# Self-attention and a circular channel filter: the sum of both channel tiles in place of x's first tile, and separate logarithms and shifts for each half of the positions

## The chip, the cores and the metric

The kernel runs on one core of one Trainium2 chip. The metric is device microseconds of one execution; the shown time is the median of three runs.

## What is computed

x has 16 images of 256 channels and 32 x 32 positions. Each image goes through a self-attention and then through a filter across channels:

```
theta = theta_w x            (32 x 1024)      phi = pool2(phi_w x)   (32 x 256)
g     = pool2(g_w x)         (128 x 256)      beta = softmax(theta^T phi)
z     = gamma * (o_w (g beta^T)) + x
out   = z + T z              T: 256 x 256, circular, 26 taps, 13 to either side
```

pool2 is the maximum over 2 x 2 positions. T plus the identity is called the band below. Because the band is circular and the channels form two tiles of 128, it has only two different blocks: the diagonal block D, the same for both tiles, and the corner block E (13 channels reach over each border), the same in both directions. So out0 = D x0 + E x1 and out1 = D x1 + E x0, with the attention part added to each.

## The kernel before

Nothing is computed in less than float32 accuracy: every operand is split into a high part (float32r, rounded) and a low part (the rest), and a product is three matmuls, high by high, high by low and low by high (`three`). Positions go in two halves h of 512 columns, channels in two tiles t (as input) or f (as output).

`over_images` runs a function `image(i, par)` on each engine, with i the pair and par the image in it. In each call PE finishes the attention of image n = (i, par) and makes the projections and scores of image n+1 (`following`). The order on each engine is written out by hand, with semaphore waits between engines:

- PE: `g_transposed` of image n (two small transposes, at the end of the call before), `scores_transposed(h)` (the probabilities' exponents, transposed, with the softmax shift as additional rows), `g_projection(n+1, h)` of 6 matmuls, `theta_phi(n+1, h)` of 4, `filter_x(h, f)` of 4 (three for the diagonal block, one for the corner: 78 stacked rows `x_edge` of the other tile), `attention_input_high/low` (4 and 2), `scores(n+1, h)`, and for each h, f `add_high_attention` (2) and `add_low_attention` (1). A turn has 64 matmuls of 512 columns, 8 of 256 and the two transposes.
- ACT: evacuations and roundings, exponentials of the scores for the sums (`exp_sums`), one logarithm of all 8 sums (`ln_sums`), `probabilities`, and `x_high`, the rounding of the image after next. It copies the results (h, f) = (1, 1) and (1, 0) out of PSUM.
- DVE: sums, pools, low parts, the maxima, the copies of (0, 1) and (0, 0) out of PSUM, and the shifts: `shifts` makes neg_max minus logarithm and its two parts (128 x 8), `turn_shifts` turns them by four 32 x 32 transposes, and `spread_shifts` writes them into rows of `theta_aug`, masked by `own_tile`, once for each half.
- POOL: `x_low` (2 a turn) and `prob_low` (2 a turn).
- SP: loads two images ahead, stores, and copies of the edge rows (`x_edges`, 6 DMAs an image).

`scores_transposed(h)` waits for the rows of `spread_shifts`; `g_transposed` waits for the evacuation of result (1, 1) of the image before, `g_projection(h=0)` for (1, 0); `theta_phi(h=1)` waits for `sum_thetaphi(h=0)`. The first two images have another order, written out separately.

Of the kernel before, what the change touches and what calls it, by code (L numbers as in the profile page):

```python
# [11 lines left out]
P = 128  # L34


def attention_then_channel_filter(nc, x, proj_wT, o_w, gamma, ring, out):
# [12 lines left out]
    K_AUG = R_SHIFT + SHIFT_ROWS  # L50
    SQUARE = 32
# [9 lines left out]
    with ExitStack() as ctx:  # L61
# [9 lines left out]
        g_raw = proj_raw[:, :, 2 * K:2 * K + CG]  # L71
        tp_w = sb("tp_w", [P, CT, 4, K], F32R)
        g_hi_w = sb("g_hi_w", [P, CT, CG], F32R)
# [8 lines left out]
        edge_w = sb("edge_w", [K_EDGE, CT * P], F32R)  # L82
        w2_hi = sb("w2_hi", [P, C], F32R)
# [40 lines left out]
        shift_turned_ps = psZ[:, 1, 4 * NT:4 * NT + P]  # L124
# [3 lines left out]
        first_ln_sum_ps = [ps[:, 1, 0:NT] for ps in scores_ps]  # L128
        first_shift_sum_ps = [ps[:, 1, NT:2 * NT] for ps in scores_ps]
# [20 lines left out]
        w2_hi_ready = sem("w2_hi_ready")  # L150
        w2_ready = sem("w2_ready")
# [51 lines left out]
        shift_turned = sem("shift_turned")  # L203
# [27 lines left out]

        def following(i, par):
            return (i, 1) if par == 0 else (i + 1, 0)
# [4 lines left out]
        def over_images(engine, image):  # L238

            image(0, 0)  # L240
            image(0, 1)
            with engine.Fori(1, PAIRS - 1) as i:
                image(i, 0)
                image(i, 1)
            image(PAIRS - 1, 0)
            image(PAIRS - 1, 1)
# [7 lines left out]
        def has_next_but_one(i, par):  # L254
            return not (is_number(i) and i == PAIRS - 1)

# [46 lines left out]
        def _(sp):  # L303
# [30 lines left out]
            def x_edges(i, par):  # L334
                for h in range(2):
                    sp.wait_ge(x_lo_ready[h], from_second(1, i, par, 1))
                stack_edges(x_edge[:, par], x_edge_loaded[par], (x_hi[:, par], x_hi[:, par], x_lo[:, par]))
# [26 lines left out]
            def image(i, par):  # L364
# [10 lines left out]
                else:  # L375
                    for h, f in ((0, 0), (0, 1), (1, 0)):
# [10 lines left out]
        def _(pool):  # L387
# [64 lines left out]

            def prob_low(i, par, h):
# [6 lines left out]
            own_tiles()  # L460
            x0_low(1, 1)
            phi0_copy(0)
            pool.wait_ge(phi0_lo_ready, 2)
# [8 lines left out]
            edge_weights()  # L472
            prob_low(0, 0, 0)
            prob_low(0, 0, 1)
            x_low(1, 0, 0)
            x_low(1, 0, 1)

            def image(i, par):
# [14 lines left out]
        def _(act):  # L493
# [5 lines left out]
            def x_high(i, par, h):  # L499
                cols = slice(h * HALF, (h + 1) * HALF)  # L500
                act.wait_ge(x_loaded[h][par], 16 * (i + par))
                if not is_second(i, par):
# [18 lines left out]
            def exp_sums(i, par, h):  # L521
                act.wait_ge(neg_max_ready, from_second(2, i, par, h + 1))
                tiles = scores_ps[h][:, :, :].rearrange("p a (b m) -> p (a b) m", m=M)
                for t in range(NT):
# [3 lines left out]
                last.then_inc(exp_sum_ready, 1)  # L528
# [72 lines left out]
            def ln_sums0(h):  # L601
                act.wait_ge(exp_sum_ready, h + 1)
                nc.scalar.activation(first_ln_sum_ps[h], exp_sum[:, h * NT:(h + 1) * NT], ACT.Ln).then_inc(ln_sum0_ready, 1)
# [40 lines left out]
            def image(i, par):  # L644
# [41 lines left out]
        def _(dve):  # L686
# [41 lines left out]
            def split_phi(i, par):  # L728
# [4 lines left out]
                else:  # L733
                    for rows in (slice(0, K), slice(2 * K, 3 * K)):
                        nc.vector.tensor_copy(phi_aug[rows, par, :], phi_pool[:]).then_inc(phi_hi_ready, 1)
# [596 lines left out]
```

## Time and profile before

| | us |
|---|---|
| median of three runs (272.91 to 273.39) | 273.18 |
| span of the profiled execution, first to last instruction | 271.3 |
| PE busy | 265.4 (98%) |
| DVE busy | 245.9 (91%) |
| ACT busy | 243.2 (90%) |
| POOL busy | 149.6 (55%) |

Busy times count an instruction from its start to its end, and neighbouring instructions of one engine overlap a little. So the work of an engine is better read from the distance between starts. About 1.9 us of the time lie outside the span.

### The profile page before, as it was taken

The numbers are of one execution on the slowest core, as the hardware profiler recorded it, in microseconds if no ns is written. First come the engines' busy times: TensorE is split into PE (matmuls) and PEld (weight loads), VectorE is DVE, ScalarE is ACT, GpSimd is POOL, SyncE is SP. The second block draws the span as 40 slices with busy tenths as digits, with TensorE's granted clock in tenths as the row PEclk, the third lists the DMA queues.
The fourth block names the chain that finished last, engine by engine and source line by source line (L and its number), as shares of the span: only waits on it lengthen the run. The fifth ranks groups of instructions, "written<-read, shape, count | busy, mean of one in ns | idle before, by whom it ended". The sixth has DMA issues, their size and how long they took to land.

```text
span 271.3 us, 4464 instructions
## 1 busy us (share of the span) xinstructions
PE 265.4 (98%) x1196; PEld 211.8 (78%) x1196; DVE 245.9 (91%) x456; ACT 243.2 (90%) x533; POOL 149.6 (55%) x79
## 2 busy tenths in 40 slices
PE   7999999999999999999999999999999999999994
PEld 3576778888888888888888888888887888888873
DVE  4998999999999999999999999999999999999953
ACT  4999999999999999998999999999999989998772
POOL 1585747574565747546673764667466475745100
PEclk9999999999999999999999999999999999999999
DMA  7978085582847657284673828467283855317044
GB/s 198 270 208 212 23 234 169 175 223 81 193 142 225 180 170 182 88 218 149 203 201 144 180 79 246 157 197 206 98 182 124 234 169 172 77 71 178 1 157 155
DMA packets 17380, 44.57 MB, mean 164 GB/s; under 512 B 2654, under 2 KB 3578, under 8 KB 16122
## 3 DMA queue, kind: packets, MB, share of 16 engines
q1 hardware_dynamic: 16682, 44.00, 56.4%
q10 hardware_dynamic: 688, 0.46, 0.5%
q8 instruction: 4, 0.07, 0.1%
q14 instruction: 6, 0.05, 0.1%
HBM read 17.45 MB, written 16.78 MB: 126 GB/s over the span
## 4 chain that ended last, share of the span: by engine, by line
PE 94%; DVE 2%; DMA 2%; ACT 0%; issue 0%; SPq 0%
PE psY L1009 10%; PE psY L988 8%; PE psY L990 7%; PE psY L989 7%; PE psV L1128 6%; PE psY L1112 6%; PE psY L1128 5%; PE psV L1112 5%; PE psV L988 3%; PE psV L990 3%; PE psV L989 3%; PE psX L1066 3%; PE psV L1096 3%; PE psV L1133 3%; PE psZ L1066 3%; PE psY L1118 3%
## 5 line engine op out<-in xcount | busy, mean ns | idle before, releaser
L457 POOL TENSOR_TENSOR prob_lo<-prob,prob_hi 128x1024 fp32r<-128x1024 f32 x30 | 72.1, 2404 | 59.7 <-ACT prob L537 32.5
L450 POOL TENSOR_TENSOR x_lo<-x_raw,x_hi 128x1024 fp32r<-128x1024 f32 x30 | 72.0, 2399 | 35.5 <-ACT x_hi L504 34.0
L504 ACT CAST x_hi<-x_raw 128x1024 fp32r<-128x1024 f32 x30 | 31.5, 1052 | 6.8 <-PE psY L1096 5.2
L526 ACT ACTIVATE psX<-psX,neg_max 128x256 f32<-128x256 f32 x60 | 26.7, 445 | 3.0 <-DVE neg_max L777 3.0
L526 ACT ACTIVATE psZ<-psZ,neg_max 128x256 f32<-128x256 f32 x60 | 27.4, 468 | 0.0
L709 DVE TENSOR_TENSOR thetaphi<-psY,thetaphi_rest 64x512 f32<-64x512 f32 x30 | 20.5, 682 | 3.8 <-ACT thetaphi_rest L508 3.1
L988 PE MATMUL psY<-x_hi,g_hi_w 128*128 128x512 f32 x56 | 22.2, 396 | 0.0
L990 PE MATMUL psY<-x_hi,g_lo_w 128*128 128x512 f32 x56 | 22.0, 393 | 0.0
L989 PE MATMUL psY<-x_lo,g_hi_w 128*128 128x512 f32 x56 | 22.0, 392 | 0.0
L715 DVE TENSOR_TENSOR theta_aug<-thetaphi,theta_aug 32x512 fp32r<-32x512 f32 x30 | 20.5, 683 | 0.9
L702 DVE TENSOR_REDUCE phi_pool<-thetaphi 32x128 f32<-32x512 f32 x30 | 20.2, 674 | 1.0
L702 DVE TENSOR_REDUCE g_pool<-psY 128x128 f32<-128x512 f32 x28 | 19.4, 692 | 0.9
L508 ACT COPY thetaphi_rest<-psY 64x512 f32<-64x512 f32 x30 | 17.5, 583 | 1.7 <-PE psY L1009 0.5
L1009 PE MATMUL psY<-x_hi,tp_w 128*128 128x512 f32 x60 | 18.9, 396 | 0.0
L777 DVE TENSOR_REDUCE neg_max<-psX 128x4 f32<-128x1024 f32 x15 | 18.3, 1217 | 0.6 <-PE psX L1050 0.6
L1009 PE MATMUL psY<-x_lo,tp_w 128*128 128x512 f32 x60 | 18.8, 394 | 0.0
L817 DVE TENSOR_TENSOR theta_aug<-psZ,own_tile 16x512 fp32r<-16x512 f32 x28 | 17.9, 678 | 0.5
L777 DVE TENSOR_REDUCE neg_max<-psZ 128x4 f32<-128x1024 f32 x15 | 18.2, 1213 | 0.0
L513 ACT CAST theta_aug<-thetaphi 32x512 fp32r<-32x512 f32 x30 | 18.1, 602 | 0.0
L519 ACT CAST theta_aug<-thetaphi 32x512 fp32r<-32x512 f32 x30 | 17.2, 617 | 0.4
L542 ACT ACTIVATE prob_hi<-psZ 128x1024 fp32r<-128x1024 f32 x16 | 16.4, 1027 | 0.4
L542 ACT ACTIVATE prob_hi<-psX 128x1024 fp32r<-128x1024 f32 x16 | 16.5, 1032 | 0.1
(189 smaller groups left out, 766.1 us busy)
## 6 DMA issues: line engine op xcount, KB each, us to landing
x_raw<-x SPq DMA_DIRECT2D x30, 512.0 KB, 5.1
out<-y SPq DMA_DIRECT2D x15, 1024.0 KB, 4.0
x_edge<-x_hi SPq DMA_DIRECT2D x64, 104.0 KB
x_edge<-x_lo SPq DMA_DIRECT2D x32, 104.0 KB
x_raw<-x SPq DMA_DIRECT2D x4, 256.0 KB, 4.5
out<-y SPq DMA_DIRECT2D x3, 256.0 KB, 2.1
band_rev<-ring SPq DMA_DIRECT2D x2, 128.0 KB, 6.9
out<-y ACTq DMA_DIRECT2D x1, 256.0 KB, 2.6
```

What stands on the lines that cost most here:

```text
L450: nc.gpsimd.tensor_tensor(x_lo[:, par, :, cols], x_raw[:, par, :, cols], x_hi[:, par, :, cols].bitcast(F32), ALU.subtract).then_inc(x_lo_r ...
L457: nc.gpsimd.tensor_tensor(prob_lo[:, h], prob[:, h], prob_hi[:, h].bitcast(F32), ALU.subtract).then_inc(prob_lo_ready, 1)
L504: nc.scalar.copy(x_hi[:, par, :, cols], x_raw[:, par, :, cols]).then_inc(x_hi_ready[h], 1)
L526: last = nc.scalar.activation(tiles[:, t, :], tiles[:, t, :], ACT.Exp, bias=neg_max[:, col:col + 1], accum_out=exp_sum[:, col:col + 1])
L542: nc.scalar.activation(prob_hi[:, h], scores_ps[h][:, :, :], ACT.Exp).then_inc(prob_hi_ready, 1)
L702: return nc.vector.tensor_reduce(dst.rearrange("p (r c) -> p r c", c=SIDE // 2), src.rearrange("p (r a c b) -> p r c a b", a=2, b=2, c=SID ...
L777: nc.vector.tensor_reduce(neg_max[:, h * NT:(h + 1) * NT], tiles, AXIS.X, ALU.max, negate=True).then_inc(neg_max_ready, 1)
L988: nc.tensor.matmul(dst, wh, vh, start=first, stop=False)
L989: nc.tensor.matmul(dst, wh, vl, start=False, stop=False)
L990: return nc.tensor.matmul(dst, wl, vh, start=False, stop=last)
L1009: last = nc.tensor.matmul(thetaphi_bank(i, par, h), tp_w[:, t].rearrange("p a k -> p (a k)"), part[:, par, t, cols], start=part is x_hi an ...
L1112: nc.tensor.matmul(o_in_bank(i, par, h), g_part[:, t, :], prob_hi[:, h, t, :], start=t == 0 and g_part is gT_hi, stop=False)
```

## The change

For all images but the first two, x0 is replaced in place by u = x0 + x1 (`add_tiles`, on POOL, once per half). With u, the sum of both outputs is S = out0 + out1 = (D + E) u, which needs no corner, and out1 = (D - E) x1 + E u. PE makes S in the bank of f = 0 and out1 in that of f = 1, and DVE writes out0 = S - out1 (`rest_of_sum`). The weights follow: for tile 1 of the projections the difference of the two tiles' weights, for S the sum of both tiles' attention weights, and the sum and difference of D and E. They are made once, by POOL, in the first 50 us. The edge rows are needed for one tile alone, so each of the 6 DMAs is half as large.

The second part: the logarithm, the shift and its parts are made for each half (`ln_half`, `half_shifts`), and a matmul by the identity (`half_shifts_to_rows`) turns each half's 8 rows, in place of the four transposes. Around this the order on ACT, DVE and PE is rewritten. One copy out of PSUM changes places: ACT takes (0, 1) in place of (1, 0), and `rest_of_sum` for h = 1 is DVE's.

```diff
+            def add_tiles(i, par, h):
+                cols = slice(h * HALF, (h + 1) * HALF)
+                pool.wait_ge(x_loaded[h][par], 16 * (i + par))
+                nc.gpsimd.tensor_tensor(x_raw[:, par, 0, cols], x_raw[:, par, 0, cols], x_raw[:, par, 1, cols], ALU.add).then_inc(u_ready[h], 1)
...
@@ POOL, image @@
-                    for h in range(2):
-                        pool.wait_ge(theta_lo_ready, upto(2, *following(i, par), h + 1))
-                        prob_low(i, par, h)
-                if has_next_but_one(i, par):
-                    for h in range(2):
+                    pool.wait_ge(theta_lo_ready, upto(2, *following(i, par), 1))
+                    prob_low(i, par, 0)
+                    pool.wait_ge(theta_lo_ready, upto(2, *following(i, par), 2))
+                    pool.wait_ge(phi_ready, from_second(1, *following(i, par), 1))
+                    prob_low(i, par, 1)
+                for h in range(2):
+                    if has_next_but_one(i, par):
                         x_low(i + 1, par, h)
+                    if has_next_but_two(i, par):
+                        ni, npar = following(i, par)
+                        add_tiles(ni + 1, npar, h)
...
@@ ACT, image @@
                     theta_high(ni, npar, 1)
+                    theta_copy(ni, npar, 0)
                 probabilities(i, par, 1)
...
-                for h in range(2):
-                    theta_copy(ni, npar, h)
+                o_in_high(i, par, 0)
+                theta_copy(ni, npar, 1)
                     x_high(i + 1, par, 0)
-                o_in_high(i, par, 0)
-                for h in range(2):
-                    exp_sums(ni, npar, h)
-                ln_sums(ni, npar)
+                out_of_psum(i, par, 0, 1)
+                exp_sums(ni, npar, 0)
+                exp_sums(ni, npar, 1, 0, 1)
+                ln_half(ni, npar, 0)
+                exp_sums(ni, npar, 1, 1, NT)
                     x_high(i + 1, par, 1)
-                for f in (1, 0):
-                    out_of_psum(i, par, 1, f)
+                ln_half(ni, npar, 1)
+                out_of_psum(i, par, 1, 1)
...
@@ DVE @@
+            def rest_of_sum(i, par, h):
+                cols = slice(h * HALF, (h + 1) * HALF)
+                dve.wait_ge(out_evacuated[h][1], upto(1, i, par, 1))
+                dve.wait_ge(out_done[h][0], upto(1, i, par, 1))
+                dve.wait_ge(y_stored[par], 16 * i)
+                nc.vector.tensor_tensor(y[:, par, 0, cols], out_bank(i, par, h, 0), y[:, par, 1, cols],
+                                        ALU.subtract).then_inc(out_evacuated[h][0], 1)
...
                 sum_thetaphi(ni, npar, 0)
+                gT_low(i, par)
                 pool_phi(ni, npar, 0)
-                gT_low(i, par)
...
-                split_phi(ni, npar)
+                round_phi(ni, npar)
                 theta_low(ni, npar, 1)
+                low_phi(ni, npar)
                 pool_g(ni, npar, 1)
+                o_in_low(i, par, 0)
                 maxima(ni, npar, 0)
-                o_in_low(i, par, 0)
                 maxima(ni, npar, 1)
-                out_of_psum(i, par, 0, 1)
                 o_in_high(i, par, 1)
-                out_of_psum(i, par, 0, 0)
+                half_shifts(ni, npar, 0)
                 o_in_low(i, par, 1)
-                shifts(ni, npar)
-                turn_shifts(ni, npar)
-                for h in range(2):
-                    spread_shifts(ni, npar, h)
+                rest_of_sum(i, par, 0)
+                half_shift_rows(ni, npar, 0)
+                half_shifts(ni, npar, 1)
+                rest_of_sum(i, par, 1)
+                half_shift_rows(ni, npar, 1)
...
@@ PE @@
+            def half_shifts_to_rows(i, par, h):
+                pe.wait_ge(half_shift_parts_ready, from_third(2, i, par, h + 1))
+                nc.tensor.matmul(half_shift_ps[h], shift_parts[:, h * NT:(h + 1) * NT, :].rearrange("p t s -> p (t s)"), ident_r[:],
+                                 start=True, stop=True).then_inc(half_shift_rows_done, 1)
...
+                last = three(out_bank(i, par, h, f), diagonal_parts, x_parts(par, f, h), True, False)
+                if f == 0 and not is_raw(i):
+                    last.then_inc(x_used[h], 1)
+                    return
...
                 g_projection(ni, npar, 1)
+                attention_input_low(i, par, 0)
                 filter_x(i, par, 0, 1)
                 scores(ni, npar, 0)
-                attention_input_low(i, par, 0)
+                add_high_attention(i, par, 0, 1)
+                add_low_attention(i, par, 0, 1)
                 scores(ni, npar, 1)
+                add_high_attention(i, par, 0, 0)
                 attention_input_high(i, par, 1)
-                for f in (1, 0):
-                    add_high_attention(i, par, 0, f)
-                add_low_attention(i, par, 0, 1)
                 attention_input_low(i, par, 1)
                 add_low_attention(i, par, 0, 0)
+                filter_x(i, par, 1, 0)
                 filter_x(i, par, 1, 1)
-                filter_x(i, par, 1, 0)
-                for f in (1, 0):
-                    add_high_attention(i, par, 1, f)
-                for f in (1, 0):
-                    add_low_attention(i, par, 1, f)
+                add_high_attention(i, par, 1, 0)
+                half_shifts_to_rows(ni, npar, 0)
+                add_high_attention(i, par, 1, 1)
+                add_low_attention(i, par, 1, 1)
+                add_low_attention(i, par, 1, 0)
...
                 g_transposed(ni, npar)
+                half_shifts_to_rows(ni, npar, 1)
```

## Rows read from the trace of the kernel before

**Rows 1.** The page: span, busy time of each engine, and PE's granted clock.
```profile
span 271.3 us, 4464 instructions
...
PE 265.4 (98%) x1196; PEld 211.8 (78%) x1196; DVE 245.9 (91%) x456; ACT 243.2 (90%) x533; POOL 149.6 (55%) x79
...
PEclk9999999999999999999999999999999999999999
```

**Rows 2.** Timeline of PE: start, duration, engine, line, operation, tiles, count.
```profile
33.04 0.38 PE L1035 MATMUL psV<-ident,g_pool 128*128 128x128 f32 x2
...
141.28 0.39 PE L988 MATMUL psV<-x_hi,band_hi 128*128 128x512 f32 x1
...
144.53 0.63 PE L1009 MATMUL psY<-x_hi,tp_w 128*128 128x512 f32 x2
...
257.83 0.38 PE L1035 MATMUL psV<-ident,g_pool 128*128 128x128 f32 x2
```

**Rows 3.** Timeline of PE at the first image's shift product.
```profile
18.88 0.22 PE L1186 MATMUL psZ<-ident_r,shift_parts 128*16 128x128 f32 x1
18.94 0.44 PE L988 MATMUL psV<-x_hi,g_hi_w 128*128 128x512 f32 x1
```

**Rows 4.** Timeline of DVE over one turn; brackets show idle time before and its releaser.
```profile
142.59 0.68 DVE L757 TENSOR_TENSOR o_in_lo<-psY,o_in_hi 128x512 fp32r<-128x512 f32 x1
...
143.78 0.90 DVE L809 STREAM_TRANSPOSE psZ<-shift_parts 32x32 f32<-32x32 f32 x4
144.72 1.28 DVE L817 TENSOR_TENSOR theta_aug<-psZ,own_tile 16x512 fp32r<-16x512 f32 x2
146.28 0.68 DVE L709 TENSOR_TENSOR thetaphi<-psY,thetaphi_rest 64x512 f32<-64x512 f32 x1 [0.28 <-ACT thetaphi_rest L508]
147.00 0.68 DVE L702 TENSOR_REDUCE phi_pool<-thetaphi 32x128 f32<-32x512 f32 x1
147.70 0.42 DVE L748 TENSOR_TENSOR gT_lo<-psV,gT_hi 128x256 fp32r<-128x256 f32 x1
148.16 0.68 DVE L715 TENSOR_TENSOR theta_aug<-thetaphi,theta_aug 32x512 fp32r<-32x512 f32 x1
148.87 0.69 DVE L702 TENSOR_REDUCE g_pool<-psY 128x128 f32<-128x512 f32 x1
...
151.04 0.94 DVE L735 CAST phi_aug<-phi_pool 32x256 fp32r<-32x256 f32 x2
152.01 0.41 DVE L737 TENSOR_TENSOR phi_aug<-phi_pool,phi_aug 32x256 fp32r<-32x256 f32 x1
152.46 0.68 DVE L715 TENSOR_TENSOR theta_aug<-thetaphi,theta_aug 32x512 fp32r<-32x512 f32 x1
```

**Rows 5.** Timeline of DVE in the first images.
```profile
21.05 0.67 DVE L709 TENSOR_TENSOR thetaphi<-psY,thetaphi_rest 64x512 f32<-64x512 f32 x1
21.65 0.67 DVE L702 TENSOR_REDUCE g_pool<-psV 128x128 f32<-128x512 f32 x1
22.36 0.68 DVE L702 TENSOR_REDUCE phi_pool<-thetaphi 32x128 f32<-32x512 f32 x1
```

**Rows 6.** Timeline of ACT at the end of the same turn.
```profile
143.40 1.05 ACT L504 CAST x_hi<-x_raw 128x1024 fp32r<-128x1024 f32 x1 [0.37 <-PE psY L1096]
```

**Rows 7.** POOL: timeline of one turn.
```profile
144.53 2.40 POOL L450 TENSOR_TENSOR x_lo<-x_raw,x_hi 128x1024 fp32r<-128x1024 f32 x1 [2.51 <-ACT x_hi L504]
149.12 2.40 POOL L457 TENSOR_TENSOR prob_lo<-prob,prob_hi 128x1024 fp32r<-128x1024 f32 x1 [2.19 <-ACT prob L537]
```

**Rows 8.** POOL: the only half-size subtraction, from the groups by line (busy, mean ns).
```profile
L407 POOL TENSOR_TENSOR x_lo<-x_raw,x_hi 128x512 fp32r<-128x512 f32 x1 | 1.3, 1263 | 5.9 <-ACT x_hi L563 5.9
```

**Rows 9.** Durations of DVE's rounding of phi: min/median/max ns.
```profile
L735 DVE CAST phi_aug<-phi_pool x28: 284/430/658, 39.0 to 248.1; 32x256 fp32r<-32x256 f32 x28
```

**Rows 10.** Timeline of the end: the last evacuation and its store.
```profile
267.57 0.58 ACT L557 COPY y<-psV 128x512 f32<-128x512 f32 x1 [0.82 <-PE psV L1133]
268.19 0.37 ACTq L665 DMA_DIRECT2D out<-y  x1
```

More of the change, by code:

```diff
@@ L241, in over_images @@
             image(0, 1)
-            with engine.Fori(1, PAIRS - 1) as i:
+            with engine.Fori(1, PAIRS - 2) as i:
                 image(i, 0)
                 image(i, 1)
-            image(PAIRS - 1, 0)
-            image(PAIRS - 1, 1)
+            for i in (PAIRS - 2, PAIRS - 1):
+                image(i, 0)
+                image(i, 1)
         def is_number(i):
@@ L255, in has_next_but_one, with has_next_but_two, is_raw @@
             return not (is_number(i) and i == PAIRS - 1)
+        def has_next_but_two(i, par):
+            return not is_number(i) or 2 * i + par + 3 < B
+        def is_raw(i):
+            return is_number(i) and i == 0
         def is_last(i, par):
@@ L519, in theta_copy, with exp_sums @@
                 nc.scalar.copy(theta_aug[K:2 * K, par, h * HALF:(h + 1) * HALF], thetaphi[0:K, h, :]).then_inc(theta_copied, 1)
-            def exp_sums(i, par, h):
+            def exp_sums(i, par, h, first=0, end=NT):
                 act.wait_ge(neg_max_ready, from_second(2, i, par, h + 1))
                 tiles = scores_ps[h][:, :, :].rearrange("p a (b m) -> p (a b) m", m=M)
-                for t in range(NT):
+                for t in range(first, end):
                     col = h * NT + t
@@ L527, in exp_sums, with ln_half @@
                                                 bias=neg_max[:, col:col + 1], accum_out=exp_sum[:, col:col + 1])
-                last.then_inc(exp_sum_ready, 1)
+                if end == NT:
+                    last.then_inc(exp_sum_ready, 1)
+            def ln_half(i, par, h):
+                act.wait_ge(exp_sum_ready, upto(2, i, par, h + 1))
+                nc.scalar.activation(half_ln_sum_ps[h], exp_sum[:, h * NT:(h + 1) * NT], ACT.Ln).then_inc(half_ln_sum_ready, 1)
             def ln_sums(i, par):
@@ L735, in split_phi, with low_phi @@
                         nc.vector.tensor_copy(phi_aug[rows, par, :], phi_pool[:]).then_inc(phi_hi_ready, 1)
+            def low_phi(i, par):
+                if not is_second(i, par):
                     dve.wait_ge(phi_hi_ready, from_second(2, i, par, 1))
@@ new lines, in half_shift_rows @@
+            def half_shift_rows(i, par, h):
+                dve.wait_ge(half_shift_rows_done, from_third(2, i, par, h + 1))
+                row = half_shift_ps[h].rearrange("r (o n) -> r o n", o=1).broadcast_to([2 * NT, NT, P])
+                own = own_tile[0:2 * NT, 0:NT].rearrange("r (t o) -> r t o", o=1).broadcast_to([2 * NT, NT, P])
+                rows = theta_aug[R_SHIFT:K_HALF, par, h * HALF:(h + 1) * HALF].rearrange("r (t n) -> r t n", n=P)
+                nc.vector.tensor_tensor(rows, row, own, ALU.mult).then_inc(shift_rows_ready, 1)
@@ L1003, in theta_phi @@
                     pe.wait_ge(thetaphi_summed, from_second(2, i, par, 1))
+                if is_number(i) and (i, par, h) == (1, 0, 0):
+                    pe.wait_ge(proj_dw_ready, 2)
+                weights = [tp_w[:, 0], tp_w[:, 1] if is_raw(i) else tp_dw[:]]
                 cols = slice(h * HALF, (h + 1) * HALF)
@@ L1022, in g_projection @@
                 for t in range(CT):
-                    last = three(g_bank(i, par, h), (g_hi_w[:, t, :], g_lo_w[:, t, :]), x_parts(par, t, h), t == 0, t == CT - 1)
+                    weights = (g_hi_w[:, t, :], g_lo_w[:, t, :]) if t == 0 or is_raw(i) else (g_hi_dw[:], g_lo_dw[:])
+                    last = three(g_bank(i, par, h), weights, x_parts(par, t, h), t == 0, t == CT - 1)
                 last.then_inc(g_done, 1)
```

173 lines of the change are left out of this document (130 added, 43 removed).

## The prediction

> **What bounds the kernel now.** I read the page first. PE is busy 98% of the span at full clock, with DVE at 91%, ACT at 90% and POOL at 55% [rows 1]: PE comes first, but two engines follow closely. The timeline of PE then gives the turn of one image. From the transposes of the second image (33.04) to those of the last (257.83) are 224.79 us and 14 turns, 16.06 each [rows 2]. Inside, 14 products of 512 columns start between 141.28 and 144.53, one each 0.232 us [rows 2]. A turn of 64 such products, 8 half-wide ones (as 4) and the transposes is 15.8 and a remainder of 0.3: PE hardly waits anywhere. So only what leaves PE's list can save time, as long as DVE and ACT keep up. The timeline of DVE shows how near DVE is: over a whole turn one marked wait of 0.28, in front of the sum at 146.28 [rows 4]. ACT shows one of 0.37, in front of the rounding of x [rows 6]. The question is thus not what PE saves, but who sets the turn afterwards.
>
> **PE alone.** The corner of f = 0 goes in 14 images and both halves: 28 products by 0.232 = 6.5 us. 28 shift products come. In the first image one of them starts at 18.88 and the next product at 18.94, which is then 0.05 longer than the usual 0.39 [rows 3]: 0.11 each, 3.1 us. Were PE all, a turn would be 16.06 - 0.46 + 0.22 = 15.82 and the kernel 3.4 us faster. The bounds of a shift product are 0.06 and 0.22, its duration [rows 3]; this moves the sum by 1.4 us down and 3.1 up.
>
> **DVE's work.** Removed are four transposes, 0.94 from start to start [rows 4]. Three small shift instructions of some 0.2 each become six, +0.6. The two copies out of PSUM become two subtractions with one operand in PSUM; the nearest row is o_in_low, 0.68 long [rows 4], which is what a copy of that size takes (0.58 on ACT [rows 10]). So DVE has 0.3 less work, a turn of some 15.4 without waits. That fits under 15.82. But DVE's new list now waits on three others within a turn: on PE for the turned rows, on ACT for each logarithm and for the evacuation of f = 1 that each subtraction reads.
>
> What a step costs on DVE I take from starts, and the rows show two kinds. Where an instruction starts on the same partitions as those before it, it begins 0.08 before the end of its forerunner: the sum at 21.05 is 0.67 long and the pool follows after 0.60 [rows 5]. Where the partitions change, or the instruction needs its forerunner's result, it begins 0.03 to 0.04 after the end: pool after 0.71 [rows 5], theta_low (0.68) followed after 0.71, gT_low (0.42) after 0.46 [rows 4]. The new order turns two of the slow steps into fast ones: gT_low stands directly behind the sum (0.60 in place of 0.72), and theta_low(1) behind the rounding of phi, whose last output starts on the same partitions (0.87 in place of 0.97 for the pair [rows 4]). No row shows the second one; its bounds are these two, and I take 0.87. The Trainium skill, VectorE: DVE Perf Modes, section "Two Vector instructions with no wait between them", has this as a rule of quadrants of 32 partitions: an instruction that starts in another quadrant than the last reads and write is held until all earlier ones have finished. Rows 4 and 5 agree with it; without the fast step the ring below would be 0.1 longer.
>
> **The ring that sets the new turn.** The new order makes a closed chain through DVE and PE. It begins with half_shift_rows(1), which needs PE's shift product of half 1, placed behind the transposes. On DVE follow, by starts: half_shift_rows 0.72 (the pair at 144.72 is 1.28 long, so one is 0.68 and a change of partitions 0.04), sum 0.60, gT_low 0.46, pool_phi 0.71, theta_low 0.71, pool_g 0.61, sum 0.72, pool_phi 0.71, rounding pair 0.87, theta_low 0.71, low_phi 0.45 (152.01 to 152.46), pool_g 0.61, and o_in_low(0) with its whole 0.68 [rows 4, 5]. That is 8.56. Then PE's add_low_attention(0, 1), which the new order has early, can go: I take 0.16, the gap of 0.04 of a dependent step and half a product for the weight load (bounds 0.04 and 0.23). From there to the transposes PE has 27 products and the scores of half 1 (as 2): 29 by 0.232 = 6.73. One shift product, 0.11, and 0.4 for the transposes and the end of the next shift product make it 7.2, and 0.04 leads back to DVE. The sum is 8.56 + 0.16 + 7.2 + 0.04 = 15.96. I add 0.04 for one of the short waits on ACT that the list has (such as the 0.28 at 146.28 [rows 4]), which makes 16.0. So not PE's 15.82, but the ring's 16.0 would be the turn: 0.06 less than now. Over the 13 turns from the third image on, -0.8 us. The other ring, from the maxima of half 0 over ACT's exponentials, x_high(1) and the second logarithm back to half_shifts(1), comes out a little shorter, by 0.1 or so.
>
> **POOL.** add_tiles is 28 additions of 1.26 each [rows 8]. With 4 instructions of 2.40 a turn [rows 7] POOL has 12.1 of 16: it fits, and the load two images ahead is there in time. Hidden, as long as add_tiles(1) is over when DVE wants to go on (see the rivals). The difference weights are made in POOL's idle time at the start: 0, at most 0.6 (half an add_tiles that ACT's x_high must wait for in the second image). I take 0, since DVE is the later one there. The halved edge copies are hidden before and after: 0.
>
> **The end.** The last image has both scores_transposed directly behind each other. The second now needs half_shift_rows(1), which starts only after the transposes and the shift product: 0.4, then 0.04 + 0.68, then 0.16, is 1.3 us after the transposes' start, and with the ring's delay up to 1.5, where PE would be ready at 0.8. +0.6. The last image's two corners are saved, -0.46. The last store was issued at 268.19, behind ACT's copy that started at 267.57 [rows 10]. Now ACT's copy is first (0.23 earlier, as PE finishes f = 1 first), and DVE's subtraction follows it: 267.34 + 0.58 + 0.04 + 0.68 = 268.64, and the issue 268.7. +0.5.
>
> **The sum.** -0.8 + 0.6 - 0.46 + 0.5 = -0.16. On the profiled execution (271.3 and 1.9 outside, 273.2) this is 273.0, and the median of the runs, 273.18, is the same time: I forecast 273.0.
>
> **Rivals.** (A) The ring is shorter than I sum it, and PE stays the bound. Its length is thirteen steps of 0.5 to 0.9 with an error of a few hundredths each; 0.15 less would do. For it: PE's list loses 0.24 and DVE's 0.3. Against it: PE is dependent on o_in_low(0) six products earlier than now. Then 13 turns by 0.24 = -3.1, -0.46 and +0.5 as above, +0.4 at the last scores: -2.7, 270.5. Halfway, 271.8.
>
> (B) Slower: add_tiles(1) holds DVE. Now x_low(1) runs from 144.53 to 146.93, and theta_low(0), with both operands in SBUF, starts at 148.16 [rows 4, 7]: 1.23 between them, where add_tiles(1) of 1.26 comes. That such overlaps cost is in the rows: the two roundings of phi that start while prob_low runs (149.12 to 151.52) take 0.94, and one alone at best 0.284; the longest took 0.658 [rows 4, 7, 9]. In the new order theta_low(0) is some 0.25 later against the transposes, so by my timeline add_tiles(1) ends 0.2 before it. If ACT's x_high(1) is later than now by more than that, theta_low(0), which stands on the ring, is held by the excess. At 0.15 a turn the 13 turns cost 2.0: 275.0. It decides from 2.9 us after the transposes' start on, as the end of add_tiles(1). The Trainium skill, SBUF — State Buffer, section "Who interferes with whom", speaks for this rival: a DVE instruction with two SBUF inputs and a GpSimd instruction that reads SBUF exclude each other, and the second one blocks fully; rows 9 agree. By it the hold would be up to the whole 1.26.
>
> (C) The ring is longer by 0.1 (theta_low(1) not early, or PE's start after a wait 0.23): 16.1, a turn as now. Then the end's +0.64 remains: 273.9.
>
> **Chances.** My forecast, with the ring between 15.96 and 16.05, 272.4 to 273.6: 0.40, a fifth of it under 272.6. (A), with what lies between: 0.33. (B) and (C) together: 0.27, nearly all over 273.7. A measurement of this kernel can tell 0.2%, 0.55 us, from no change. Faster 0.41, same 0.33, slower 0.26. The range takes in (A) whole and (B) at 0.15: 270.3 to 275.3.
>
> **What the profile would show.** PE has 28 corner products fewer and some marked waits on DVE o_in_lo in front of add_low_attention(0, 1), none now; the distance of the transposes is 16.0 (15.8 in A, over 16.1 in B). DVE waits in front of o_in_high(1) and half_shifts. half_shift_rows(1) starts 0.4 to 0.5 after the transposes. In (B) theta_low is longer than 0.68 on the mean, or idle before it. At the end the last DVE instruction is a subtraction behind ACT's copy. I am wrong if the turn is under 15.9 or over 16.1.

## The result and the profile after

The changed kernel takes 277.80 us (median of 4 runs, 277.70 to 277.85) beside 273.28 for the kernel before on the same chip: a ratio of 1.0148, 95% interval 1.0113 to 1.0183 (the two medians alone give 1.0165, inside it). The forecast was 273.0 with a range up to 275.3; the time lies above it. The page of the changed kernel, answering to [rows 1]:

```profile
span 276.1 us, 4480 instructions
...
PE 266.0 (96%) x1196; PEld 205.7 (74%) x1196; DVE 244.3 (88%) x442; ACT 245.6 (89%) x547; POOL 191.3 (69%) x120
...
PEclk9999999999999999999999999999999999999999
...
L515 POOL TENSOR_TENSOR x_raw<-x_raw 128x512 f32<-128x512 f32 x28 | 36.6, 1308 | 0.0
```

The granted clock is full and PE's busy time hardly moved, yet its share fell from 98% to 96%: PE now waits somewhere. POOL is the engine with much more work, 41.7 us, 36.6 of it the 28 additions of the tiles (1308 ns each on the mean, where the estimate was 1.26 us). The first thing to find is where in the span the 4.8 us are. The transposes of g stand once in each turn, so their starts on PE's timeline cut the span into pieces, as in [rows 2]:

```profile
35.08 0.44 PE L1150 MATMUL psV<-ident,g_pool 128*128 128x128 f32 x2
...
53.05 0.38 PE L1150 MATMUL psV<-ident,g_pool 128*128 128x128 f32 x2
...
69.22 0.38 PE L1150 MATMUL psV<-ident,g_pool 128*128 128x128 f32 x2
...
261.60 0.38 PE L1150 MATMUL psV<-ident,g_pool 128*128 128x128 f32 x2
```

| | before | after | difference |
|---|---|---|---|
| first image's transposes | 16.24 | 16.67 | +0.43 |
| from there to the second image's | 16.80 | 18.41 | +1.61 |
| first turn, to the third image's | 16.19 | 17.97 | +1.78 |
| the 13 turns from there | 208.60 | 208.55 | -0.05 |
| last transposes to the end | 13.47 | 14.50 | +1.03 |
| span | 271.3 | 276.1 | +4.8 |

So 3.82 of 4.8 us are lost before the third image's transposes, 1.03 at the end, and nothing on balance in the thirteen turns that the prediction spent most of its words on.

**The start.** PE's marked waits from 20 us to the third image's transposes, in the changed kernel:

```profile
23.40 0.50 PE L1099 MATMUL psV<-x_hi,band_hi 128*128 128x512 f32 x1 [0.91 <-DVE w_lo L998]
...
27.08 0.71 PE L1165 MATMUL psX<-phi_aug,theta_aug 96*128 96x256 f32 x4 [0.53 <-DVE phi_aug L830]
...
44.72 0.72 PE L1165 MATMUL psX<-phi_aug,theta_aug 96*128 96x256 f32 x4 [1.04 <-DVE phi_aug L830]
```

They name DVE, and DVE is not idle there: single instructions of it are far too long (w_lo in the rows is what `w2_low` writes). DVE's timeline of the changed kernel at the first and third of these places:

```profile
21.09 2.25 DVE L998 TENSOR_TENSOR w_lo<-w_raw,w_hi 128x256 fp32r<-128x256 f32 x1
...
40.91 2.51 DVE L825 CAST phi_aug<-phi_pool 32x256 fp32r<-32x256 f32 x2
```

The same two places in the kernel before:

```profile
20.66 0.47 DVE L894 SCALAR_TENSOR_TENSOR w_lo<-psV,gamma_sb,w_hi 128x256 fp32r<-128x256 f32 x1
...
39.03 0.89 DVE L735 CAST phi_aug<-phi_pool 32x256 fp32r<-32x256 f32 x2
```

And POOL's timeline of the changed kernel says what ran meanwhile:

```profile
20.67 2.38 POOL L521 TENSOR_TENSOR prob_lo<-prob,prob_hi 128x1024 fp32r<-128x1024 f32 x1 [0.34 <-ACT prob L625]
...
36.98 1.31 POOL L515 TENSOR_TENSOR x_raw<-x_raw 128x512 f32<-128x512 f32 x1
38.24 0.94 POOL L502 TENSOR_TENSOR band_c<-band 128x128 f32<-128x128 f32 x1
39.14 0.46 POOL L503 TENSOR_TENSOR band_c<-band 128x128 f32<-128x128 f32 x1
39.56 2.40 POOL L521 TENSOR_TENSOR prob_lo<-prob,prob_hi 128x1024 fp32r<-128x1024 f32 x1
41.93 1.34 POOL L515 TENSOR_TENSOR x_raw<-x_raw 128x512 f32<-128x512 f32 x1
```

w2_low used to read its product from PSUM and took 0.47 us. In the changed kernel both its inputs lie in SBUF; it starts 0.42 after prob_low(0, 0, 0), and ends at 23.34, 0.29 after prob_low does (23.05). The two roundings of phi start at 40.91 inside prob_low(0, 1, 0), which comes late because three additions stand ahead of it, and end only after the addition that follows it on POOL has run as well. This is rival (B)'s mechanism, at places where the prediction did not look.

The 0.43 that are already there at the first image's transposes come from one more such place, at 6 us. The first two rows are DVE's and POOL's in the changed kernel, the last is DVE's in the kernel before:

```profile
6.08 1.12 DVE L931 TENSOR_TENSOR x_lo<-x_raw,x_hi 128x512 fp32r<-128x512 f32 x1 [0.41 <-ACT x_hi L651]
```

```profile
6.07 0.59 POOL L477 TENSOR_TENSOR proj_d<-proj_raw 128x192 f32<-128x192 f32 x1 [3.98 <-DMA proj_raw<-proj_wT]
```

```profile
6.13 0.69 DVE L827 TENSOR_TENSOR x_lo<-x_raw,x_hi 128x512 fp32r<-128x512 f32 x1 [0.43 <-ACT x_hi L563]
```

The POOL instruction is the difference of the projections' weights, which the prediction put at 0. In every changed kernel below it runs beside this low part of x, which then takes 0.87 to 1.12; in the two kernels without it, 0.69. No experiment moved it. So the 3.82 read as 0.43 here, 1.61 mainly at w2_low (1.78 too long), and 1.78 in the first turn (the roundings are 1.62 too long).

**The turn.** DVE's timeline of one changed turn, from half_shift_rows(1) to o_in_low(0), and PE's product that waits for it; it answers to [rows 4]:

```profile
150.04 0.68 DVE L921 TENSOR_TENSOR theta_aug<-psZ,own_tile 8x512 fp32r<-8x512 f32 x1
150.76 0.68 DVE L799 TENSOR_TENSOR thetaphi<-psY,thetaphi_rest 64x512 f32<-64x512 f32 x1
151.37 0.41 DVE L841 TENSOR_TENSOR gT_lo<-psV,gT_hi 128x256 fp32r<-128x256 f32 x1
...
152.51 0.68 DVE L805 TENSOR_TENSOR theta_aug<-thetaphi,theta_aug 32x512 fp32r<-32x512 f32 x1
...
155.25 1.03 DVE L825 CAST phi_aug<-phi_pool 32x256 fp32r<-32x256 f32 x2
156.20 0.68 DVE L805 TENSOR_TENSOR theta_aug<-thetaphi,theta_aug 32x512 fp32r<-32x512 f32 x1
...
157.97 0.68 DVE L850 TENSOR_TENSOR o_in_lo<-psV,o_in_hi 128x512 fp32r<-128x512 f32 x1
```

```profile
158.70 0.50 PE L1264 MATMUL psY<-o_in_lo,w_hi 128*128 128x512 f32 x1
```

From 150.04 to the end of o_in_low(0), 158.65, are 8.61; the prediction had 8.56. PE follows 0.05 later. theta_low(0) is 0.68, not held. This is a turn of 16.15; in every other one the first rounding is 0.14 shorter and the same stretch is 8.46 long. The waits of the changed kernel, in total, times and longest:

```profile
PEld psY L1264 <- DVE o_in_lo L850: 5.1, 14, 0.4
```

PE waits 0.36 in each turn at the forecast place.

**The end.** PE's second scores of the last image, first in the kernel before, then in the changed one, and then the last evacuations of the changed one:

```profile
258.51 0.65 PE L1066 MATMUL psZ<-theta_aug,phi_aug 112*128 112x512 f32 x2
```

```profile
262.94 0.73 PE L1188 MATMUL psZ<-theta_aug,phi_aug 104*128 104x512 f32 x2 [0.39 <-DVE theta_aug L921]
...
271.63 0.59 ACT L645 COPY y<-psV 128x512 f32<-128x512 f32 x1 [0.81 <-PE psV L1264]
272.25 0.69 DVE L866 TENSOR_TENSOR y<-psY,y 128x512 f32<-128x512 f32 x1 [0.71 <-ACT y L645]
```

The second scores start 1.34 after the transposes (0.68 before), +0.66. The last evacuation is the subtraction behind ACT's copy, as forecast.

### The profile page after: what moved, and what is told of

The parts are those of the page before. It is cut to its first block, busy times and chain, and to the rows that moved or that the text cites. A ratio compares the mean times of both kernels' runs of the same rounds, so it can differ in the third digit from the quotient of the medians.

```text
span 276.1 us, 4480 instructions
## 1 busy us (share of the span) xinstructions
PE 266.0 (96%) x1196; PEld 205.7 (74%) x1196; DVE 244.3 (88%) x442; ACT 245.6 (89%) x547; POOL 191.3 (69%) x120
## 4 chain that ended last, share of the span: by engine, by line
PE 84%; DVE 11%; DMA 2%; issue 1%; ACT 1%; SPq 0%; DVEq 0%
PE psY L1123 9%; PE psY L1099 7%; PE psY L1100 7%; PE psY L1101 7%; PE psV L1258 6%; PE psY L1258 5%; PE psY L1241 5%; PE psV L1241 4%; PE psY L1264 3%; PE psX L1165 3%; PE psV L1264 3%; PE psZ L1165 3%; PE psY L1247 3%; PE psV L1101 3%; PE psV L1099 3%; PE psV L1100 3%
## 5 line engine op out<-in xcount | busy, mean ns | idle before, releaser
L515 POOL TENSOR_TENSOR x_raw<-x_raw 128x512 f32<-128x512 f32 x28 | 36.6, 1308 | 0.0
L602 ACT CAST theta_aug<-thetaphi 32x512 fp32r<-32x512 f32 x30 | 18.6, 620 | 0.7
L596 ACT CAST theta_aug<-thetaphi 32x512 fp32r<-32x512 f32 x30 | 18.1, 602 | 0.5 <-DVE thetaphi L799 0.5
L846 DVE CAST o_in_hi<-psY 128x512 fp32r<-128x512 f32 x15 | 10.4, 691 | 8.9 <-PE psY L1247 8.9
L625 ACT ACTIVATE prob<-psZ 128x1024 f32<-128x1024 f32 x16 | 16.5, 1029 | 0.4
L625 ACT ACTIVATE prob<-psX 128x1024 f32<-128x1024 f32 x16 | 16.2, 1012 | 0.0
L825 DVE CAST phi_aug<-phi_pool 32x256 fp32r<-32x256 f32 x28 | 14.4, 513 | 0.9
L609 ACT ACTIVATION_READ_ACCUMULATOR psZ<-psZ,neg_max 128x1 f32 x60 | 13.7, 228 | 0.0
```

The costliest lines, as they stand in the source:

```text
L515: nc.gpsimd.tensor_tensor(x_raw[:, par, 0, cols], x_raw[:, par, 0, cols], x_raw[:, par, 1, cols], ALU.add).then_inc(u_ready[h], 1)
L609: last = nc.scalar.activation(tiles[:, t, :], tiles[:, t, :], ACT.Exp, bias=neg_max[:, col:col + 1], accum_out=exp_sum[:, col:col + 1])
L625: nc.scalar.activation(prob[:, h], scores_ps[h][:, :, :], ACT.Exp).then_inc(prob_ready, 1)
```

## The experiments

Twelve kernels. Beside the medians, one table by piece of the span, since an edit of the start is seen best there; each row is one profiled execution. The kernel names are those of the headings below. "Lock" in them means a DVE instruction that is held by POOL's. In the executions shown for "band earlier", "tail" and "all moves" x landed late and the first image's transposes are 1.0 to 1.4 late, so their second column has to be read less the first.

```
                     first      third      the turn  mean of the   last transposes
                     image's    image's    after it  next 12       to the end
before               16.24      49.23      16.03     16.05         13.47
after                16.67      53.05      16.17     16.03         14.50
w2_low from PSUM     16.45      51.88      16.16     16.04         14.44
band earlier         17.66      53.41      16.15     16.04         14.48
both                 16.47      51.29      16.16     16.05         14.55
one later            16.66      50.50      16.77     16.05         14.57
later still          16.73      50.27      17.58     16.04         14.45
start light          16.54      49.74      16.87     16.05         14.44
lock in before       16.41      50.82      16.03     16.04         13.52
o_in_low first       16.53      52.70      15.92     15.96         14.61
extra off            16.48      52.85      16.18     16.06         14.57
extra on             16.66      53.06      16.37     16.23         14.50
tail                 18.07      54.42      16.18     16.04         13.93
all moves            17.73      51.54      16.49     16.00         13.69
```

### w2_low from PSUM, band_combined earlier, and both

The first kernel gives w2_low its PSUM operand back:

```diff
-  nc.vector.tensor_tensor(w2_lo[:], w2_raw[:], w2_hi[:].bitcast(F32), ALU.subtract)
+  nc.vector.scalar_tensor_tensor(w2_lo[:], w2_ps, gamma_sb[:, 0:1], w2_hi[:].bitcast(F32),
+                                 ALU.mult, ALU.subtract)
```

> The changed kernel with one instruction of the start undone: w2_low again reads the product from PSUM and only w2_hi from SBUF. Everything else, the steady turns included, is as changed. Theory L (VectorE and GpSimd exclude each other where a VectorE instruction has two SBUF inputs): the 2.25 us instruction goes back to 0.47, the second image's transposes start 1.7 to 1.9 us earlier, about 276.0. Theory Q (what was lost is the queue on POOL, w2_high and the additions in front of other work): the instruction's operands do not matter, 277.6 to 277.9.

The second makes the two band sums on POOL earlier, away from prob_low(0, 1, 0) (the expectations of the later kernels call this edit "band_combined later"; it is the one shown here):

```diff
   add_tiles(1, 0, 1)
+  band_combined()
   x_low(1, 0, 1)
   add_tiles(1, 1, 0)
-  band_combined()
```

> The changed kernel with band_combined (two POOL additions of 128x128) in front of x_low(1,0,1), where POOL waits for ACT, and no longer in front of prob_low(0,1,0). Theory L: prob_low(0,1,0) begins 0.6 to 1.3 us earlier, the rounding of phi that stood behind it falls from 2.51 us for the pair to about 1.0 to 1.5, and the first turn from 17.97 to about 16.5: 276.3 to 276.9. Theory D (the first turn is long because DVE is late there from the start): same time as the change, 277.8.

The third has both edits.

> Both edits together. Theory L: they add, 274.3 to 275.0, and what is left over the kernel before is the end (1.0) and the first 10 us (0.4). A theory in which the steady turns lost the time says no better than 277.

Measured: 276.88 (276.73 to 277.01; ratio 1.0124, 1.0092 to 1.0156) for the first, 277.72 (277.21 to 278.47; 1.0150, 1.0115 to 1.0186) for the second, 276.27 (276.10 to 277.32; 1.0108, 1.0081 to 1.0135) for both. None reached what was expected (about 276.0; 276.3 to 276.9; 274.3 to 275.0). In the first, w2_low is short again, but the one that comes next into POOL's way is not. DVE's timeline of the kernel with w2_low from PSUM:

```profile
20.86 0.47 DVE L998 SCALAR_TENSOR_TENSOR w_lo<-psV,gamma_sb,w_hi 128x256 fp32r<-128x256 f32 x1
...
23.26 1.39 DVE L805 TENSOR_TENSOR theta_aug<-thetaphi,theta_aug 32x512 fp32r<-32x512 f32 x1
```

and POOL's of the same kernel:

```profile
20.44 2.40 POOL L521 TENSOR_TENSOR prob_lo<-prob,prob_hi 128x1024 fp32r<-128x1024 f32 x1 [0.36 <-ACT prob L625]
...
22.81 1.29 POOL L515 TENSOR_TENSOR x_raw<-x_raw 128x512 f32<-128x512 f32 x1
```

w_lo starts 0.42 into prob_low here too, and takes 0.47: with one operand in PSUM it is not held. theta_low(0, 1, 0), two inputs in SBUF, starts 0.45 into add_tiles(1, 0, 0) and takes 1.39 in place of 0.68. So 1.8 us of holding gone gave back 1.2 on the third image's transposes and 0.9 of the time. In the second kernel the first turn is 17.33 in place of 17.97, while its two roundings of phi still take 1.87: now prob_low(0, 1, 0) is early again, but add_tiles(1, 1, 1) directly behind it takes POOL's turn before DVE's second rounding. Its profiled execution began 1.0 later, with x landing late (the tail kernel below shows such a row). Its four times lie in two pairs, 277.2 and 278.2 to 278.5; the median between them is its rival's figure and says little, but even the faster pair is 0.6 under the changed kernel, not the 0.9 to 1.5 expected. Both edits together gave 1.5, not the 3 that the theory of two holds expected: the mechanism stands, the count of the places was wrong.

### The lock put into the kernel before

```diff
+  nc.vector.tensor_scalar(w2_raw[:], w2_ps, gamma_sb[:, 0:1], None, ALU.mult)
+  nc.vector.tensor_copy(w2_hi[:], w2_raw[:])
-  nc.vector.scalar_tensor_tensor(w2_lo[:], w2_ps, gamma_sb[:, 0:1], w2_hi[:].bitcast(F32),
-                                 ALU.mult, ALU.subtract)
+  nc.vector.tensor_tensor(w2_lo[:], w2_raw[:], w2_hi[:].bitcast(F32), ALU.subtract)
```

> The kernel before with one thing of the change alone: DVE writes w2 unrounded to SBUF, rounds it there, and makes w2_low from the two SBUF tiles in place of from PSUM. Theory (DVE and POOL exclude each other when DVE has two inputs in SBUF): w2_low starts at about 20.9 while POOL's prob_low(0, 0, 0) runs from 20.24 to 22.65; it is about 1.8 long in place of 0.47, PE waits about 1 us in front of the band products of the first image, and the kernel takes 274.3 to 275.0. Rival (DVE just has one small instruction more, and the loss of the change at this place comes from PE's new order): w2_low stays near 0.5 long, 273.3 to 273.7.

Measured: 274.57 (10 runs, 274.31 to 274.75), ratio 1.0039 (1.0020 to 1.0058). DVE's row, then POOL's, then PE's wait, in this kernel:

```profile
21.16 1.92 DVE L898 TENSOR_TENSOR w_lo<-w_raw,w_hi 128x256 fp32r<-128x256 f32 x1
```

```profile
20.41 2.38 POOL L459 TENSOR_TENSOR prob_lo<-prob,prob_hi 128x1024 fp32r<-128x1024 f32 x1 [0.47 <-ACT prob L539]
```

```profile
PEld psV L991 <- DVE w_lo L898: 1.0, 1, 1.0
```

With nothing else of the change, the instruction takes 1.92, ends 0.29 after prob_low, PE waits 1.0, and the kernel takes 1.3 more by the medians (1.1 by the ratio, 0.5 to 1.6 by its interval). That is inside what was expected, and the rival, a w2_low near 0.5 long, is out. DVE's added rounding, 0.33 from start to start, can be a part of the 1.3; the hold is 1.45.

### One addition later, two later, and a start without them

The kernel "one later" is "both" with add_tiles(1, 1, 1) moved; "later still" also moves w2's sum:

```diff
   prob_low(i, par, 0)
-  if is_second(i, par):
-      add_tiles(1, 1, 1)
   ...
   prob_low(i, par, 1)
+  if is_second(i, par):
+      add_tiles(1, 1, 1)
```

```diff
   add_tiles(1, 0, 0)
-  w2_sum()
   ...
   band_combined_parts()
+  w2_sum()
```

> The changed kernel with three moves, nothing left out: w2_low from PSUM, band_combined later, add_tiles(1, 1, 1) behind prob_low(0, 1, 1); w2's sum is left where the change has it. Theory (each POOL instruction that leaves DVE's way at one place is in the way at the next, or late): the turn from the second to the third image's transposes is 16.4 in place of 17.3, but the next is longer than 16.16, by the hold of theta_low at about 53 or a late x_low; together 275.7 to 276.3. Rival (the holds can be cleared one by one): 275.3 or less.

> The changed kernel with four moves on POOL and DVE, nothing left out: w2_low from PSUM, band_combined later (both as before), and now add_tiles(1, 1, 1) behind prob_low(0, 1, 1) and w2's sum into the second image's turn. Theory: the rounding of phi at about 39.8 is no longer held a second time (1.87 down to about 1.2) and theta_low(0, 1, 1) at 25.7 is 0.68 again; the hold of theta_low(0, 1, 0) by add_tiles(1, 0, 0), 0.7, stays. 275.3 to 275.8. Rival: the hold moves on to the next instruction of DVE, or POOL is late for x: 276.2 or more.

Measured: 276.29 (275.89 to 276.82; ratio 1.0110, 1.0087 to 1.0134) and 276.76 (276.48 to 277.58; 1.0125, 1.0083 to 1.0167). In both the two roundings are back at 0.88 and 0.89 and the first turn at 16.32 and 16.35, close to the 16.19 of before. But the next turn pays. In "one later" DVE's theta_low is held by the addition for the fifth image, which POOL comes to later (DVE's row, then POOL's):

```profile
53.44 1.20 DVE L805 TENSOR_TENSOR theta_aug<-thetaphi,theta_aug 32x512 fp32r<-32x512 f32 x1
```

```profile
52.81 1.28 POOL L515 TENSOR_TENSOR x_raw<-x_raw 128x512 f32<-128x512 f32 x1
```

In "later still" the same instruction is held (1.22), here by x_low, which is now late itself, on PE's timeline:

```profile
53.94 0.50 PE L1124 MATMUL psY<-x_lo,tp_w 128*128 128x512 f32 x1 [0.74 <-POOL x_lo L470]
```

The first was expected at 275.7 to 276.3 with the next turn longer: met. That of the second, 275.3 to 275.8, was missed on the side of its rival.

"Start light" asks what is left without the additions. It has w2_low from PSUM, the two moves of the last kernel, and adds only 4 columns of each tile for the third and fourth image, which leaves that part of the computation out:

```diff
-  cols = slice(h * HALF, (h + 1) * HALF)
+  cols = slice(h * HALF, (h * HALF + 4) if is_number(i) and i == 1 else (h + 1) * HALF)
```

> The changed kernel, with w2_low from PSUM, w2's sum made only in the second image's turn, and the four additions of the tiles for the third and fourth image cut to 4 columns each (so these two images are filtered with wrong sums; that part of the computation is left out). Theory (the whole loss of the start is POOL's new work holding DVE): the third image's transposes start at 49.7 to 50.3 in place of 53.05, 274.6 to 275.2. Rival (at least half of the loss is PE's own longer list and DVE's new order of the second image): no more than what the earlier run without the w2 lock and with band_combined later gave, 276.0 to 276.5.

Measured: 275.51 (275.32 to 275.92; ratio 1.0066, 1.0032 to 1.0100), more than the 274.6 to 275.2 expected. The place is met: the third image's transposes start at 49.74. The windows of 20 to 54 us, in order the kernel before, the changed one, and this one (length; busy time and count of PE, PEld, DVE, ACT, POOL; PE's granted clock, DMA's busy share, GB/s):

```profile
20.00:54.00 34.00, 33.80 (x154) 26.31 (x153) 31.59 (x57) 32.27 (x70) 20.23 (x9) 1.00 0.56 162
```

```profile
20.00:54.00 34.00, 31.48 (x141) 23.40 (x140) 31.21 (x51) 29.45 (x66) 29.69 (x21) 1.00 0.41 119
```

```profile
20.00:54.00 34.00, 33.80 (x154) 26.01 (x153) 30.87 (x54) 32.20 (x71) 25.53 (x22) 1.00 0.49 151
```

PE is as busy, with as many products, as in the kernel before. The remaining 0.51 at this point are 0.30 at the first image's transposes, where the low part of x beside the weights' difference still takes 1.04, and 0.23 in the first turn, which has two shift products, 2 x 0.11. Several edits are in this kernel at once, so it shows that POOL's new work at these places makes up the loss, not how much each piece does. What made the total miss is the turn after: w2's sum, moved into it, pushes POOL's next addition onto theta_low again (1.41 long at 52.68), and that turn is 16.87.

### An extra product off the ring and on it

```diff
   if f == 0 and not is_raw(i):
+      if h == 0 and has_next(i, par):        # the second kernel: h == 1
+          last = nc.tensor.matmul(out_bank(i, par, h, f), idle_operand[:, 0:P],
+                                  x_hi[:, par, 1, h * HALF:(h + 1) * HALF], start=False, stop=False)
       last.then_inc(x_used[h], 1)
```

> The changed kernel with one product of 512 columns more on PE (zero weights, so it adds nothing to the result) in filter_x(0, 0) of images 3 to 15, which stands ahead of the place where PE waits for o_in_lo(0). Theory (the turn is a ring through DVE, PE has 0.2 to 0.4 to spare in front of o_in_lo): the wait in front of add_low_attention(0, 1) shrinks from 0.4 to about 0.15 and the kernel stays at 277.8 to 278.2. Rival (PE's own list sets the turn): 13 x 0.232 = 3.0 more, 280.8.

> The same extra product, but in filter_x(1, 0), which PE comes to behind add_low_attention(0, 1) and ahead of the transposes and of the shift product of half 1. Theory of the ring: this stretch of PE is part of it, the turn is 0.23 longer, 13 x 0.232 = 3.0, 280.8. Rival (another engine alone sets the turn, DVE or ACT by its work): under 1 more, 278 to 278.7.

Measured: 278.01 (277.71 to 278.05; ratio 1.0167, 1.0146 to 1.0188) off the ring, and 280.38 (280.09 to 281.29; 1.0264, 1.0238 to 1.0290) on it. The wait for o_in_lo, first in the kernel off, then on the ring:

```profile
PEld psY L1267 <- DVE o_in_lo L850: 1.6, 6, 0.4
```

```profile
PEld psY L1267 <- DVE o_in_lo L850: 5.0, 14, 0.4
```

Thirteen products of 0.232 more cost 0.2 where PE waits behind them anyway, and 2.6 where it doesn't (3.0 was expected). So PE's sum doesn't set the turn; a product counts where the ring passes.

### o_in_low(0) first

```diff
-  pool_g(ni, npar, 1)
   o_in_low(i, par, 0)
+  pool_g(ni, npar, 1)
   maxima(ni, npar, 0)
```

> The changed kernel, where DVE makes o_in_low(0) before pool_g(1) in each turn; the start is untouched. Ring theory (the turn of 16.04 is set by the chain half_shift_rows(1) to o_in_low(0) to PE and back): the chain is 0.4 shorter, PE's wait of 0.36 a turn before add_low_attention(0,1) goes, and the turn falls to 15.82 to 15.95: 275 to 276.5. PE theory (the turn is PE's own list): no change, 277.8.

Measured: 276.52 (276.21 to 276.74; ratio 1.0110, 1.0078 to 1.0143), at the slow end of what the ring was expected to give. One DVE step of 0.61 is taken out of the ring and the turn falls by only 0.07. The waits of this kernel show who took over:

```profile
PEld psV L1150 <- ACT y L645: 2.7, 13, 0.3
```

```profile
DVE psX L907 <- ACT psX L616: 5.4, 14, 0.4
```

PE no longer waits for o_in_lo in the turn; DVE waits for the logarithm of half 0 and the transposes for ACT's evacuation. That a chain over ACT's exponentials, like the other ring of the prediction (which went by the second logarithm), now sets the turn is read from these waits; no run tests it.

### The tail, and all moves together

```diff
   if is_last(i, par):
-      scores_transposed(i, par, 1)
       filter_x(i, par, 0, 1)
+      scores_transposed(i, par, 1)
```

> The changed kernel with one swap on PE in the last image: filter_x(0, 1), four products, stands in front of scores_transposed(1), which has to wait for half_shift_rows(1). Theory (the end lost 0.4 there): the wait of 0.39 is gone, 277.3 to 277.5. Rival (the end is set by DVE and ACT behind the last products, and the wait costs nothing): 277.8, or more, since the probabilities of half 1 come later.

Measured: 277.84 (277.41 to 278.76; ratio 1.0149, 1.0109 to 1.0190): in the median nothing, where 277.3 to 277.5 was expected. The piece of the span does show it: from the last transposes to the end are 13.93 in place of 14.50. The profiled execution is the one of 278.76, and it began late; PE's timeline of it:

```profile
9.41 1.04 PE L1274 MATMUL psY<-x_raw,proj_raw 128*64 128x512 f32 x2 [1.05 <-DMA x_raw<-x]
```

This wait for the first image is absent in the changed kernel's profile. So a gain of 0.57 at the end is seen in one execution, and not resolved in the runs.

The last kernel has the edits of "one later", "o_in_low first" and "tail", and the shift product of half 1 ahead of the transposes.

> All moves together: w2_low from PSUM, band_combined and add_tiles(1, 1, 1) later, o_in_low(0) ahead of pool_g(1) on DVE, half_shifts_to_rows(1) ahead of the transposes on PE, and in the last image filter_x(0, 1) ahead of the second scores. If the three places of loss (start, ring, end) add up as the runs with one of them gave: 276.0 less 1.3 for the ring and 0.4 to 0.6 for the end, 274.0 to 274.6, not faster than before. Rival (with o_in_low early and the shift product ahead of the transposes PE is the bound, turn 15.85): 13 x 0.15 less, 272 to 273.

Measured: 274.61 (6 runs, 274.52 to 275.49), ratio 1.0046 (1.0030 to 1.0062), as the sum of the single gains had it; the rival's turn of 15.85 did not come (16.00). What the moved shift product gives by itself isn't known. Most of the loss is undone, and the change still doesn't pay.

## Why the prediction was wrong

**The step that failed is the start**, "the difference weights are made in POOL's idle time at the start: 0, at most 0.6", with "POOL ... hidden" beside it. With the first turn it cost 3.82. The argument was about POOL's time (12.1 of 16 us a turn) and not about what POOL holds while it works. Four things were missed. First, the prediction does not speak of w2_low, while the diff turns its PSUM operand into an SBUF one; alone in the kernel before that costs 1.3, at most 0.3 of it for the added rounding (shown). Second, the difference of the projections' weights holds the low part of x at 6 us, for the 0.43 (read from the traces, not tested); the size is inside the 0.6 that the prediction allowed, but it had another cause in mind, ACT waiting for an addition. Third, the additions for the third and fourth image all fall into a stretch where POOL also has the band's and w2's sums. Fourth, "13 turns from the third image on" left out the first turn, which has the two shift products (+0.22) and no corner product less. With the additions cut to 4 columns, w2_low from PSUM, and w2's sum and add_tiles(1, 1, 1) later, 3.3 of the 3.82 are gone (shown). What clearing each hold would give can't be added up singly, as each cleared one let DVE or POOL run into the next.

**Rival (B) named the right mechanism and the wrong place.** It placed the hold at theta_low(0) of every turn, with the rule of the Trainium skill, SBUF — State Buffer, section "Who interferes with whom", beside it. In the steady turn theta_low stays 0.68: add_tiles(1) runs 150.87 to 152.18 and theta_low starts at 152.51, 0.33 later, where the prediction had a margin of 0.2. What remains in the turn is small: in every second image the roundings start 1.84 after prob_low(0) and take 1.03, in the others 1.98 after it and take 0.89, and the turns alternate between 16.01 and 16.15. At the start the rule holds for a subtraction with two SBUF inputs: the second of the two is held until the first has ended (w2_low, 2.25 and 1.92, both ending 0.29 after prob_low). Rows 9, which the prediction called in agreement with it, are roundings with one SBUF input; they show a hold, but not of that kind of instruction. The chance given to slower (0.26) was too low because the mechanism was tried at one place only.

**The turn** was forecast at 16.0 by the ring, and the ring is what sets it. In the changed kernel it reads 0.48 from the transposes to half_shift_rows(1), 8.46 or 8.60 on DVE, 0.06 to PE's start and 7.02 from there to the next transposes: 16.02 and 16.16, for turns of 16.01 and 16.15. That PE alone (15.82) doesn't decide is shown by the pair of extra products. The size was a little off: the way from PE's start over the transposes back to DVE is 7.50 (7.02 and 0.48) where the sum had 7.24, PE's start 0.06 for 0.16, and DVE 8.53 on the mean for 8.56. That eats the 0.06 of gain. The twelve turns are 0.2 shorter in all only because the last of them, where the last image's corner is left out, is 15.75 beside 16.02; the other eleven take 176.63 beside 176.55. The turn after the third image's transposes is 0.14 longer, so the -0.8 became -0.05. Rival (A) is out. Of rival (C) the size came true, a turn as now, but not its causes: theta_low(1) starts 0.08 before the end of the roundings (156.20, they end at 156.28), as taken, and PE starts at once after its wait.

**The end** was forecast at +0.64 and measured +1.03. The scores' delay is 0.66 (0.6 forecast) and the last evacuation 0.51 (0.5 forecast): from the last product's start to the end are 4.67 us in place of 4.16. The corners are the step that was off: the last image's second corner product stands ahead of the transposes and is in the turn before (15.75 long), so of the 0.46 only half belongs here, and 0.09 of that is lost behind the wait.

## What to carry to other kernels

Before moving work to an idle POOL, list DVE's instructions with two SBUF inputs, and its SBUF roundings, that would run at the same time, stage by stage and the start above all, since each may be held until the POOL instruction ends. Check in the diff which operand of a DVE instruction moves from PSUM to SBUF: that alone can make it four times as long. And where a turn is a ring through two engines, an engine's saved products count only if they lie on the ring.

## What the runs showed of the hardware

- A DVE subtraction of 128x256 that starts 0.42 after a POOL subtraction of 2.4 us takes 0.47 with one operand in PSUM, and 2.25 with both in SBUF, at the same place of the same list.
- A rounding with one SBUF input is held as well: two of 32x256 took 2.51, 1.87 or 0.89, by what POOL ran beside them.
- A held instruction ended at the same distance behind POOL's each time: a rounding of 32x256 0.15 (before, after, "both"), a subtraction of 128x256 0.29 (after, "lock in before"), one of 32x512 0.55 ("w2_low from PSUM", "one later"). The wait is inside its duration and not shown as idle time.
- When POOL's instruction ends and another stands directly behind it, DVE gets one instruction in and its next is held again (the 1.87 of "both", from 39.78: prob_low from 37.80, add_tiles from 40.17 to 41.50).
- POOL is held too: the sum of the band took 0.94 at 38.24, beside DVE's theta_low of 38.17, and the like sum directly after, beside none, 0.46.
- The first image's x can land a microsecond later in one execution than in another, and it shifts the whole span; pieces between two events of PE are then the better measure.
